# Two groups of rows per step in an attention kernel on one core: like TensorE blocks side by side, and work moved between engines

## What is computed

```python
xn = (x - moving_mean) * rsqrt(moving_var + 0.001) * gamma + beta
q, k, v = xn @ Wq + bq, xn @ Wk + bk, xn @ Wv + bv
scores = einsum('bhid,bhjd->bhij', q, k) * 64 ** -0.5
out = einsum('bhij,bhjd->bhid', softmax(scores, axis=-1), v) @ Wo + bo
return xn + out
```

## Time and profile before

| | us |
|---|---|
| median of 3 runs | 5052.27 |
| lowest, highest | 5052.20, 5053.69 |
| the profiled execution | 5052.57 |
| its span in the profile | 5050.8 |

### The profile page before, as it was taken

The page is one execution under the profiler, slowest core; times in us unless marked ns, Lnnn a source line. Parts: engine busy times, 40 slices in busy tenths (PEclk is TensorE's granted clock), DMA queues, the critical chain, the costliest instruction groups (busy, mean ns, idle before and its releaser), DMA issues.

```text
span 5050.8 us, 171699 instructions
## 1 busy us (share of the span) xinstructions
PE 5017.7 (99%) x51224; PEld 4097.2 (81%) x51224; DVE 4168.3 (83%) x8226; ACT 4619.3 (91%) x19460; POOL 4860.0 (96%) x3080
## 2 busy tenths in 40 slices
PE   7999999999999999999999999999999999999999
PEld 6888888888888888888888888888888888888887
DVE  6888888888888888888888888888888888888887
ACT  7999999999999999999999999999999999999998
POOL 7999999999999999999999999999999999999998
PEclk9999999999999999999999999999999999999999
DMA  7888888888888888888888888888888888888886
GB/s 136 161 161 161 161 161 161 161 161 161 160 161 160 161 161 161 161 161 161 161 161 160 162 160 161 161 160 161 160 161 161 161 161 161 161 161 161 161 161 136
DMA packets 4294235, 806.26 MB, mean 160 GB/s; under 512 B 4294208, under 2 KB 4294208, under 8 KB 4294208
## 3 DMA queue, kind: packets, MB, share of 16 engines
q1 hardware_dynamic: 4294208, 805.93, 82.2%
HBM read 537.10 MB, written 268.44 MB: 159 GB/s over the span
## 4 chain that ended last, share of the span: by engine, by line
PE 99%; issue 0%; DVE 0%; SPq 0%; POOL 0%; ACT 0%; DMA 0%; POOLq 0%; DVEq 0%; ACTq 0%
PE score_ps L494 22%; PE u_ps L505 21%; PE probsT_ps L481 21%; PE g_ps L521 17%; PE o_ps L540 14%; PE o_ps L529 4%; POOL y L263 0%; DMA bias_col<-in_L_conv_bv 0%; ACT probs L294 0%; PE u_ps L470 0%; SPq L180 0%; SPq L178 0%; SPq L182 0%; ACT g L316 0%; POOL x_weighted L254 0%
## 5 line engine op out<-in xcount | busy, mean ns | idle before, releaser
L294 ACT ACTIVATE probs<-score_ps,neg_top 128x128 f32<-128x128 f32 x8192 | 2935.6, 393 | 2.5 <-DVE neg_top L426 2.5
L254 POOL TENSOR_TENSOR x_weighted<-x_in,row_weights 128x1024 f32<-128x1024 f32 x1024 | 2424.9, 2368 | 173.0 <-POOL x_scaled_rows L270 66.8
L294 ACT ACTIVATION_READ_ACCUMULATOR probs<-score_ps,neg_top 128x1 f32 x8192 | 1894.7, 231 | 0.0
L407 DVE TENSOR_REDUCE row_stat<-score_ps 128x8 f32<-128x1024 f32 x1024 | 1255.4, 1226 | 353.2 <-PE score_ps L494 353.2
L263 POOL TENSOR_TENSOR y<-attn,x_scaled_rows 128x512 f32<-128x512 f32 x1024 | 1307.6, 1277 | 13.6 <-DVE attn L401 13.6
L481 PE MATMUL probsT_ps<-ident,probs 128*128 128x128 f32 x8192 | 1286.5, 280 | 0.7 <-ACT probsT L308 0.7
L270 POOL TENSOR_TENSOR x_scaled_rows<-x_weighted,out_bias 128x512 f32<-128x512 f32 x1024 | 1224.2, 1196 | 0.4
L494 PE MATMUL score_ps<-xT,g 64*128 64x128 f32 x16384 | 1190.8, 285 | 2.0 <-ACT g L316 2.0
L505 PE MATMUL u_ps<-probsT,x_in 128*64 128x128 f32 x16384 | 1120.5, 279 | 0.0
L494 PEld LDWEIGHTS score_ps<-xT,g 64*128 64x128 f32 x16384 | 994.6, 187 | 128.4 <-ACT g L316 5.3
L401 DVE TENSOR_TENSOR attn<-o_ps,inv_sum 128x512 f32<-128x512 f32 x1024 | 707.9, 691 | 467.1 <-DVE inv_sum L446 391.9
(11 more groups left out here) (66 smaller groups left out, 1843.2 us busy)
## 6 DMA issues: line engine op xcount, KB each, us to landing
x_quads<-in_x SPq DMA_DIRECT2D x4096, 64.0 KB, 2.2
x_in<-in_x SPq DMA_DIRECT2D x1024, 256.0 KB, 2.9
out<-y SPq DMA_DIRECT2D x1024, 256.0 KB, 2.7
norm_row<-in_L_conv_gamma SPq DMA_DIRECT2D x1, 32.0 KB, 3.7
norm_row<-in_L_conv_beta SPq DMA_DIRECT2D x1, 32.0 KB, 3.7
norm_row<-in_L_conv_moving_mean SPq DMA_DIRECT2D x1, 32.0 KB, 4.2
norm_row<-in_L_conv_moving_var SPq DMA_DIRECT2D x1, 32.0 KB, 4.4
norm_row<-in_L_conv_bo SPq DMA_DIRECT2D x1, 32.0 KB, 4.7
```

The source lines that it names most:

```text
L254: nc.gpsimd.tensor_tensor(x_weighted[:, n % 2, :, 0:2 * C].rearrange("p s (h c) -> p s h c", h=2), x_in[:, n % 8, :, None, :].broadcast_to ...
L294: last = nc.scalar.activation(probs[:, n % 2, q, :], score_ps[n % 2][:, q // PAIRS, q % PAIRS * W:(q % PAIRS + 1) * W], ACT.Exp, bias=neg_ ...
L407: nc.vector.tensor_reduce(row_stat[:, s, :, ROW_MAX].rearrange("p (h k) -> p h k", h=2), score_ps[n % 2][:].rearrange("p h (k w) -> p h k ...
```

## The change

One step now handles two groups of 8 rows, 2t and 2t+1, in each stage, and the loop body has 8 such steps (`BODY` 16).

- PE does both groups' scores, then both groups' P x, and then everything that uses the whole array.
- P x of the odd group is written to the output's bank, now `uo_ps`; copied out of there before the even group's output is written.
- DVE handles in one instruction for both groups: the constants, the transpose of x, the reciprocals.
- DVE takes over the copy of the second four transposes of the even group. For the odd group, it scales the output in place in PSUM and adds `x_scaled_rows` into y itself; POOL adds y only for even groups.
- Loads run up to 9 groups ahead, and most buffers have twice the slots.

```diff
-BODY = 8
+BODY = 16
...
-        x_in = sb("x_in", [128, 8, GROUP, C])
+        x_in = sb("x_in", [128, 16, GROUP, C])
...
-        xT = sb("xT", [128, 4, PAIRS, W])
+        xT = sb("xT", [128, 8, PAIRS, W])
...
-        probs = sb("probs", [128, 2, GROUP, W])
+        probs = sb("probs", [128, 4, GROUP, W])
...
-        u_ps, g_ps, probsT_ps, o_ps = (psum(n) for n in ("u_ps", "g_ps", "probsT_ps", "o_ps"))
+        u_ps, g_ps, probsT_ps, uo_ps = (psum(n) for n in ("u_ps", "g_ps", "probsT_ps", "uo_ps"))
...
             def step(r, t, peeled):
-                load_quads(r, t + 4, peeled)
-                load(r, t + 4, peeled)
-                store(r, t - 3, peeled)
+                for n in (2 * t + 8, 2 * t + 9):
+                    load_quads(r, n, peeled)
+                    load(r, n, peeled)
+                store(r, 2 * t - 5, peeled)
+                store(r, 2 * t - 6, peeled)
...
+                weigh(r, 2 * t + 4, peeled)
+                add_bias(r, 2 * t + 3, peeled)
+                weigh(r, 2 * t + 5, peeled)
+                add_x(r, 2 * t - 6, peeled)
+                add_bias(r, 2 * t + 4, peeled)
```

`weigh`, `add_bias` and `add_x` are POOL's three operations of before, each as a function. ACT's new step; `keep_probsT` with half 0 or 1 and `keep_g` are the copies of before:

```diff
+            def step(r, t, peeled):
+                exponentials(r, 2 * t, peeled, range(0, 6))
+                keep_probsT(r, 2 * t - 2, peeled, 0)
+                exponentials(r, 2 * t, peeled, range(6, 7))
+                keep_g(r, 2 * t + 4, peeled)
+                exponentials(r, 2 * t, peeled, range(7, 8))
+                exponentials(r, 2 * t + 1, peeled, range(0, 4))
+                keep_probsT(r, 2 * t - 1, peeled, 0)
+                exponentials(r, 2 * t + 1, peeled, range(4, 8))
+                keep_g(r, 2 * t + 5, peeled)
+                keep_probsT(r, 2 * t - 1, peeled, 1)
```

DVE's; `scale_first`, `find_max`, `find_shift` (the two small sums) and `keep_u` are operations of before as functions:

```diff
+            def scale_and_add_second(r, n, peeled):
...
+                dve.wait_ge(sum_inverted[s], uses(r, n))
+                dve.wait_ge(o_made[s], uses(r, n))
+                nc.vector.tensor_tensor(o_rows, o_rows, inv_sum[:, s, :, None].broadcast_to([128, GROUP, C]),
+                                        ALU.mult).then_inc(o_scaled[s], 1)
+                dve.wait_ge(o_scaled[s], uses(r, n))
+                dve.wait_ge(x_scaled[s], uses(r, n))
+                if exists(r, n - 4, peeled):
+                    dve.wait_ge(y_stored[s], dma_uses(r, n - 4))
+                nc.vector.tensor_tensor(y[:, s], o_rows, x_scaled_rows[:, n % 16], ALU.add).then_inc(y_found[s], 1)
...
             def step(r, t, peeled):
+                scale_and_add_second(r, 2 * t - 5, peeled)
+                find_max(r, 2 * t, peeled)
+                find_shift(r, 2 * t, peeled)
+                find_max(r, 2 * t + 1, peeled)
+                keep_u(r, 2 * t - 4, peeled, u_ps)
+                keep_u(r, 2 * t - 3, peeled, uo_ps)
+                find_shift(r, 2 * t + 1, peeled)
+                n = 2 * t + 3
...
+                    nc.vector.tensor_reduce(row_stat[:, s - 1:s + 1, :, ROW_CONST], x_weighted[:, s - 1:s + 1, :, C:2 * C + 1],
+                                            AX_X, ALU.add).then_inc(const_found[s], 1)
+                n = 2 * t - 2
...
+                    dve.wait_ge(probsT_b_made[s], uses(r, n))
...
+                    nc.vector.tensor_copy(probsT[:, n % 2, HALF:GROUP, :], probsT_rows).then_inc(probsT_b_kept[s], 1)
+                scale_first(r, 2 * t - 4, peeled)
+                n = 2 * t + 7
...
+                    nc.vector.transpose(xT[:, n % 8 - 1:n % 8 + 1].rearrange("p g k w -> p (g k w)"),
+                                        x_quads[:, s - 1:s + 1].rearrange("p g k w -> p (g k w)")).then_inc(xT_kept[s], 1)
+                n = 2 * t - 1
...
+                    dve.wait_ge(probs_b_found[s], uses(r, n))
+                    nc.vector.reciprocal(inv_sum[:, s - 1:s + 1, :], prob_sum[:, s - 1:s + 1, :]).then_inc(sum_inverted[s], 1)
```

PE's; the functions are the blocks of before, with these waits where they are new:

```diff
+            def probs_times_x(r, n, peeled, bank):
...
+                pe.wait_ge(probsT_a_kept[s], uses(r, n))
+                pe.wait_ge(probsT_b_kept[s], uses(r, n))
+                if exists(r, n - 2, peeled):
+                    if bank is uo_ps:
+                        pe.wait_ge(y_found[parts(n - 2)], uses(r, n - 2))
+                    else:
+                        pe.wait_ge(u_kept[parts(n - 2)], uses(r, n - 2))
...
+            def output(r, n, peeled, pairs):
...
+                if 0 in pairs:
+                    pe.wait_ge(u_kept[s], uses(r, n))
+                    if n % 2 == 0:
+                        pe.wait_ge(u_kept[parts(n + 1)], uses(r, n + 1))
+                    else:
+                        pe.wait_ge(attn_kept[parts(n - 1)], uses(r, n - 1))
...
+            def step(r, t, peeled):
+                scores(r, 2 * t, peeled)
+                scores(r, 2 * t + 1, peeled)
+                probs_times_x(r, 2 * t - 4, peeled, u_ps)
+                probs_times_x(r, 2 * t - 3, peeled, uo_ps)
+                transpose_probs(r, 2 * t - 2, peeled, 0)
+                project(r, 2 * t + 4, peeled)
+                output(r, 2 * t - 4, peeled, range(0, 1))
+                transpose_probs(r, 2 * t - 2, peeled, 1)
+                output(r, 2 * t - 4, peeled, range(1, PAIRS))
+                project(r, 2 * t + 5, peeled)
+                transpose_probs(r, 2 * t - 1, peeled, 0)
+                output(r, 2 * t - 3, peeled, range(0, PAIRS))
+                transpose_probs(r, 2 * t - 1, peeled, 1)
```

More of the change, by code:

```diff
@@ new lines, in _, with scores @@
+            o_pairs = uo_ps[:].rearrange("p (h k c) -> p h k c", h=2, k=PAIRS)
+            def scores(r, n, peeled):
+                if not exists(r, n, peeled):
+                    return
+                s = parts(n)
+                pe.wait_ge(g_kept[s], uses(r, n))
+                if exists(r, n - 2, peeled):
+                    pe.wait_ge(probs_b_found[parts(n - 2)], uses(r, n - 2))
+                for k in range(PAIRS):
+                    for h in range(2):
+                        half = slice(h * C, (h + 1) * C)
+                        last = nc.tensor.matmul(score_ps[n % 2][:, h, k * W:(k + 1) * W], g[half, s, k, :],
+                                                xT[half, n % 8, k, :], start=True, stop=True)
+                last.then_inc(scores_made[s], 1)
@@ new lines, in probs_times_x @@
+            def probs_times_x(r, n, peeled, bank):
+                if not exists(r, n, peeled):
+                    return
+                s = parts(n)
+                pe.wait_ge(probsT_a_kept[s], uses(r, n))
+                pe.wait_ge(probsT_b_kept[s], uses(r, n))
+                if exists(r, n - 2, peeled):
+                    if bank is uo_ps:
+                        pe.wait_ge(y_found[parts(n - 2)], uses(r, n - 2))
+                    else:
+                        pe.wait_ge(u_kept[parts(n - 2)], uses(r, n - 2))
+                for k in range(PAIRS):
+                    for h in range(2):
+                        last = nc.tensor.matmul(bank[h * C:(h + 1) * C, k * W:(k + 1) * W], x_in[:, n % 16, PAIRS * h + k, :],
+                                                probsT[:, n % 2, PAIRS * h + k, :], start=True, stop=True)
+                last.then_inc(u_made[s], 1)
@@ L511, in step, with transpose_probs @@
+            def transpose_probs(r, n, peeled, half):
+                if not exists(r, n, peeled):
+                    return
+                s = parts(n)
+                if half == 0:
                     pe.wait_ge(probs_a_found[s], uses(r, n))
@@ L544, in _, with project @@
-            pipeline(pe, step, dma=True)
+                for q in range(HALF):
+                    last = nc.tensor.transpose(probsT_ps[:, q * W:(q + 1) * W], probs[:, n % 4, half * HALF + q, :], ident[:])
+                last.then_inc((probsT_a_made if half == 0 else probsT_b_made)[s], 1)
+            def project(r, n, peeled):
+                if not exists(r, n, peeled):
+                    return
+                s = parts(n)
+                pe.wait_ge(xT_kept[parts(n | 1)], uses(r, n | 1))
+                if exists(r, n - 1, peeled):
+                    pe.wait_ge(g_kept[parts(n - 1)], uses(r, n - 1))
+                nc.tensor.matmul(g_ps[:], w_g_all, xT[:, n % 8].rearrange("p k w -> p (k w)"),
+                                 start=True, stop=True).then_inc(g_made[s], 1)
@@ new lines, in output @@
+            def output(r, n, peeled, pairs):
+                if not exists(r, n, peeled):
+                    return
+                s = parts(n)
+                if 0 in pairs:
+                    pe.wait_ge(u_kept[s], uses(r, n))
+                    if n % 2 == 0:
+                        pe.wait_ge(u_kept[parts(n + 1)], uses(r, n + 1))
+                    else:
+                        pe.wait_ge(attn_kept[parts(n - 1)], uses(r, n - 1))
+                for k in pairs:
+                    last = nc.tensor.matmul(o_pairs[:, :, k, :], uT[:, n % 2, k, :], w_o_all, start=True, stop=True)
+                if PAIRS - 1 in pairs:
+                    last.then_inc(o_made[s], 1)
```

324 lines of the change are left out of this document (135 added, 189 removed).

## The result

The changed kernel takes 5486.02 us (median of 4 runs, 5479.6 to 5488.85) against 5052.24 (4 runs): ratio 1.0856 [1.0837, 1.0875], **8.6% slower**. Forecast was 4972, range 4885 to 5045.

The account below looks back on a forecast made before the run. PE's own sequence was taken as the bound. 512 steps of 9.60 us gave 4915.2; ends of 43.4 + 11.2 made a span of 4969.8, and 1.8 beyond the span gave 4972 us, range 4885 to 5045.

Parts of the forecast that it names:

- the part on SP: SP's loads, stores and the added register operations on sequencers: claimed to cost nothing.
- a slower sequencer would show as "issue": Sign given for added register operations costing time after all: "issue" in the profile.
- the ends: Time outside the steady steps, at start and drain: 43.4 us before, plus 11.2 (5 to 17) for the change.
- Three changes of arrangement fewer, 0.50: PE switches array arrangement three times instead of six per 16 rows: 0.50 us saved.
- The path of waits, 9.60: PE's 16-row period, followed through its waits: 9.60 us, with 0.32 of the 0.50 given back to ACT's two copies.
- Rival 1: PE alone sets the period, 9.28 us per 16 rows: 4808 us in all; chance 0.09.
- The in-place scale, 0.69: DVE's scaling of the odd group's output in PSUM: taken as attn's 0.69 us, bounds 0.68 and 1.26.
- rival 2: In-place scale ties DVE to PE: at its 1.26 upper bound, period 9.93, 5141 us, slower; chance 0.10.
- the 1.23 that was taken: DVE's paired constants: duration taken from the maximum's row, 1.23 us long; the paired transpose's upper end was 1.24.
- The rule that I set against the move to DVE: Skill's advice: ScalarE near PSUM, VectorE near SBUF; it would put the scale above 0.69, toward rival 2.
- POOL and ACT off the path: POOL's dropped y add worth nothing in itself; ACT, work 9.0 to 8.5, not the bound, though its order can be.
- its cover: Loads queued behind SP's stores are wanted two steps later, so waiting stores cost nothing; without it DVE's transpose and PE wait.

Follow-up runs that it names:

- e5: e4 with SP issuing a step's loads of x first, then the stores of the step before, then its small loads: 5489.24 us, ratio 1.0862.
- e6: e5 with PE's loop body at 8 groups instead of 16: 5016.74 us, ratio 0.9927.
- e7: e6 with all engines' bodies at 8 groups, x_scaled_rows in 8 slots and POOL's bias two groups later: 4998.67 us, ratio 0.9892.
- e10: Kernel before with the same two extra passes a step as e9, but at 64 rows: 5634.54 us, ratio 1.115.
- e9: Kernel before with two extra PE passes a step at 128 rows, behind a first transpose: 5280.38 us, ratio 1.045.
- e8: e7 with ACT's copy of the even group's first transposes after five exponentials instead of six: 4934.38 us, ratio 0.9765.
- e4: Changed kernel with 8 instead of 16 slots for x, its loads issued four groups later: 7154.81 us, ratio 1.4163.
- e12: Kernel before with a loop body of 16 groups on PE alone, the other engines at 8: 5349.89 us, ratio 1.0586.
- e14: Kernel before, body of 8 groups, score and P x matmuls each issued twice (1312 tensor instructions a round): 6863.58 us.
- e15: Kernel before, body of 8 groups, score and P x matmuls each issued three times (1824 tensor instructions a round): 9256.87 us.
- e1: Kernel before with loop bodies of 16 groups on all engines, nothing else changed: 5371.09 us, ratio 1.0625.
- e2: Kernel before with loop bodies of 16 groups on SP, POOL, ACT and DVE, PE staying at 8: 5088.29 us, ratio 1.0068.

## Why the prediction was wrong, point by point

- **The step that failed** is in the part on SP: "Added register operations run on sequencers that are ahead of their engines: nothing". I looked at what the doubled loop body adds to a step, and not at the body itself: 1600 tensor instructions on PE in place of 800. It costs 472.5 (e5 to e6), and the other engines' bodies at most some 18 (e6 to e7, which also moves POOL's bias). No rival named it. The rival on the slower side was the in-place scale, so its 0.10 was held for a wrong mechanism. The term that the sum put at nothing measured 7.9 at each return of the loop. The sentence did name the sign, "a slower sequencer would show as 'issue'", and so it shows.
- **The sum closes.** Forecast 4972; the step of 9.648 in e7 (415 of them from 500.97 to 4504.95) instead of 9.60, 512 times: +25; the ends +2, which is what is left of e7; the other engines' code +18; PE's code +472.5; e5 over the changed kernel -3: 5486.
- **Three changes of arrangement fewer, 0.50**: right. Two score blocks take 1.99 where twice 1.10 was, two P x blocks 1.90 where twice 1.02 was, and the price of a change is shown apart from all else (e10 over e9).
- **The path of waits, 9.60**: right within 0.05 (9.65), the copies of ACT as the two waits; e8 shows that the first is a wait for the copy, by moving it. Rival 1 (PE alone, 9.28) isn't reached by any version.
- **The in-place scale, 0.69**: right. The group of the page of the changed kernel, with the paired transpose and the paired constants:

```profile
L435 DVE TENSOR_TENSOR uo_ps<-uo_ps,inv_sum 128x512 f32<-128x512 f32 x512 | 358.1, 699 | 122.4 <-PE uo_ps L610 122.4
...
L504 DVE STREAM_TRANSPOSE xT<-x_quads 128x1024 f32<-128x1024 f32 x512 | 631.9, 1234 | 2.1 <-DMA x_quads<-in_x 2.1
L487 DVE TENSOR_REDUCE row_stat<-x_weighted 128x16 f32<-128x1040 f32 x512 | 629.7, 1230 | 2.4 <-POOL x_weighted L260 2.4
```

  0.699 against attn's 0.69 with its output in SBUF, so writing PSUM cost DVE next to nothing here (0.01) and rival 2 falls. The paired pieces are the 1.23 that was taken. The rule that I set against the move to DVE (the Trainium skill, Advanced Engine Details and Errata, The Read-Write Bubble) shows no penalty on this write.
- **POOL and ACT off the path**: right (85% and 86% busy in e7; ACT idle 1.13 on average before its first exponential, released by the small sum). SP: right for the change, and e4 shows what its cover is worth when the order of the queue is touched.
- **Left open**: where between 1312 and 1600 the edge lies and what sets it; why the clock falls behind most heads and not behind the 9 of e12, whose waits are as long; what the second wait of the changed kernel's heads is, behind 19 of the 32 score passes; which engine's code q14 carries.

## What to carry to other kernels

When a change unrolls a loop further or makes its body longer, count the instructions of a round on the engine that bounds, and read the instruction queues on the page: a few packets for the whole program mean that the loop stays in, packets that grow with the rounds mean a fetch at each head, and a stall there if they are the bounding engine's. A gain per step must be compared with a price per round: here 8 steps gain 0.13 each, 1.1 in all, and a return costs 7.9. And when two versions differ in loop length and in order of work, make the one that differs in length alone first: it costs one run.

## What the runs showed of the hardware that was not expected

- A loop body of 1312 tensor instructions on PE showed no wait at the branch (e14); 1600 (e12) and 1824 (e15) cost 4.9 and 4.7 a return in the kernel before and 1600 cost 7.9 in the changed one (e5 over e6), with 9 packets of 16 KB fetched at each.
- The fetch is only part of the price. PE idle for 3.38 was followed by a granted clock of 0.50 (1.2 GHz) while it worked again, which made the score passes and the first P x up to twice as long and stretched waits of 4.58 (3.38 and 1.20) to a loss of 7.56. It isn't so every time: in e12 a head that waited 2.87 kept the clock at 1.00 and lost 2.93, one that waited 3.36 had 0.50 and lost 6.22.
- The other engines' bodies of 16 groups were fetched again too (5 packets of 8 KB a return on q14 in e1 and e2), for only 0.6 a return in e2, where PE was the bound.
- Two passes at 64 rows between passes at 128 cost PE 0.35 more than two at 128 (e10 over e9), 0.17 a change on average, at the 2.4 GHz level, with nothing to wait for.
